# A graph layer on one core: edges sorted without gaps (831 gathers for 880 pairs), matmuls that find their chunk by registers, and a smaller routing sort

## What is computed

```python
def _hconv(x, W, b, src, dst, n):
    xt = x @ W
    m = segment_sum(xt[src], dst, n) * Binv[:, None]
    out = segment_sum(m[dst], src, n) * Dinv[:, None]
    return out + b
# graph part: two _hconv with a prelu; beside it a linear attention over all rows;
# behind both a normalization and a mixture of 8 experts, 2 of them weighted per row:
h = gelu(xn @ W1[e] + b1[e]); y += (h @ W2[e] + b2[e]) * w_full[..., e]
```

## Time and profile before

| | us |
|---|---|
| median of 3 runs | 6197.29 (6196.83 to 6203.05) |
| the profiled execution, time / span | 6198.35 / 6196.6 |
| mean granted TensorE clock | 0.841 |
| busy: PE / DVE / ACT / POOL | 4354.5 / 3632.5 / 1291.3 / 4050.3 |
| start to the first gather | 647 |
| pass 0, 1, 2, 3 with the stretch behind each | 1177, 1170, 1147, 1120 |
| normalization and scores | 237 |
| routing, of it the sort's loop | 157, 131 |
| experts, final sums | 470, 71 |

### The profile page before, as it was taken

One profiled execution on the slowest core, in us unless ns is written; L12 is line 12 of the kernel. 1 busy time (PEld: TensorE's weight loads), 2 busy tenths in 40 slices (PEclk: granted clock), 3 DMA queues, 4 the chain that ended last, 5 costly groups with the idle time before them and its releaser, 6 DMA issues.

```text
span 6196.6 us, 63953 instructions
## 1 busy us (share of the span) xinstructions
PE 4354.5 (70%) x16894; PEld 2841.8 (46%) x16895; DVE 3632.5 (59%) x10972; ACT 1291.3 (21%) x3391; POOL 4050.3 (65%) x4182
## 2 busy tenths in 40 slices
PE   4899799999957777675466565645565555647995
PEld 1555455555534444443244444424433333545663
DVE  7887788888846666665555555544444444443223
ACT  0587455555500000000100000000000000212442
POOL 2777777777757777777577777767777776003442
PEclk8999899999968888997777877777787776757997
DMA  3400333333353333334444444473333335200114
GB/s 116 126 1 1 85 104 104 103 103 103 104 127 112 112 112 111 112 112 94 131 137 139 136 137 138 128 191 109 105 105 105 105 105 98 90 27 29 61 62 158
DMA packets 331514, 641.97 MB, mean 104 GB/s; under 512 B 82320, under 2 KB 201700, under 8 KB 330704
## 3 DMA queue, kind: packets, MB, share of 16 engines
q0 software_dynamic: 191808, 490.67, 29.4%
q1 hardware_dynamic: 131652, 139.90, 6.9%
q10 hardware_dynamic: 7756, 7.97, 0.4%
HBM read 551.23 MB, written 87.01 MB: 103 GB/s over the span
## 4 chain that ended last, share of the span: by engine, by line
PE 46%; DVE 14%; issue 13%; POOL 8%; DMA 8%; ACT 1%; DVEq 1%; ACTq 0%; SPq 0%; POOLq 0%; PEldq 0%
PE PS L1367 27%; POOL gbuf L538 8%; DVE acc L946 7%; DMA gbuf<-table,idx 7%; PE PS L1335 6%; PE PS L1544 3%; PE PS L1567 3%; PE PS L1397 2%; DVE ohg L955 2%; PE PS L1524 1%; PE PS L1560 1%; PE PS L1435 1%; DMA gbuf<-ye_d 1%; PE PS L1492 1%; DVE gbuf L1194 0%
## 5 line engine op out<-in xcount | busy, mean ns | idle before, releaser
L538 POOL DMA_INDIRECT gbuf<-table,idx x3520 | 3364.4, 956 | 1184.1 <-issue 810.6
L1367 PE MATMUL PS<-gbuf,ohg 128*128 128x257 f32 (+1 forms) x7040 | 2273.6, 469 | 1383.0 <-issue 760.4
L1367 PEld LDWEIGHTS PS<-gbuf,ohg 128*128 128x128 f32 x7040 | 1539.5, 231 | 2108.3 <-issue 1323.4
L946 DVE TENSOR_TENSOR acc<-acc,PS 128x257 f32 (+1 forms) x3520 | 1492.8, 424 | 1715.2 <-PE PS L1367 1692.8
L955 DVE TENSOR_SCALAR ohg<-iota,dl 128x128 f32<-128x128 f16 x2640 | 813.7, 315 | 86.4 <-issue 86.4
L1335 PE MATMUL PS<-region 128*128 128x440 f16 x3328 | 687.3, 349 | 0.0
L546 POOL DMA_INDIRECT scattered_d<-acc x384 | 373.7, 973 | 127.1 <-issue 121.0
L1335 PEld LDWEIGHTS PS<-region 128*128 128x128 f16 x3328 | 324.5, 97 | 282.7 <-issue 1.6
L640 ACT ACTIVATE region<-region,acc 128x128 f16<-128x128 f16 x832 | 334.0, 401 | 522.6 <-DVE region L897 516.3
L896 DVE TENSOR_SCALAR region<-iota_c,acc 128x880 f16<-128x880 f16 x832 | 411.0, 494 | 23.2 <-issue 23.2
L1335 PE MATMUL PS<-acc,region 128*128 128x440 f16 x1792 | 335.3, 350 | 7.7 <-ACT region L641 7.7
(11 more groups left out here) (284 smaller groups left out, 3570.6 us busy)
## 6 DMA issues: line engine op xcount, KB each, us to landing
gbuf<-table,idx POOLq DMA_INDIRECT x3520, 2.8
table<-acc SPq DMA_DIRECT2D x21, 896.0 KB, 6.7
region<-xt_d SPq DMA_DIRECT2D x98, 128.0 KB, 2.2
gbuf<-ye_d SPq DMA_DIRECT2D x12, 1024.0 KB, 7.6
xpad_d<-acc SPq DMA_DIRECT2D x1, 6272.0 KB, 22.0
xn_d<-acc SPq DMA_DIRECT2D x49, 128.0 KB
xt_d<-acc SPq DMA_DIRECT2D x49, 128.0 KB
table<-acc SPq DMA_DIRECT2D x49, 128.0 KB
```

The source lines that it names most:

```text
L538: gp.indirect_dma_start(gbuf[:, c % U, 0:F], None, tables[p], bass.IndirectOffsetOnAxis(idx[p % 2][:, c:c + 1], 0)).then_inc(s_g[c % U // ...
L946: TT(a, a, chunk_sum(p, k), ALU.add).then_inc(s_acc[p], 1)
L1367: m = MM(chunk_sum(p, k), ohg[:, k, :], gbuf[:, k, 0:width(p)], start=True, stop=True)
```

## The change

- A block no longer begins a new chunk. Edges lie without gaps: CH = 831 chunks. A chunk in which a new block begins is used once for each block; such a use is a pair. Pair w reads chunk w minus the number of blocks begun before it; there are 879 at most, PAIR = 880. Gathers run over CH, one-hots, matmuls and adds over PAIR.
- The lane numbers per pair are made on the chip: transposes, a spreading by matmul (`stairs`, `turn_keys`, `spread_keys`, `lanes`), for order 0 ahead of pass 0, for order 1 in the last turns of pass 0.
- Gathered rows go to a ring of 58 (passes 0, 2) or 64 (1, 3) columns that takes `gbuf` and space of the idle accumulator. TensorE finds a pair's chunk by a register, 16 loaded per turn.
- Gather c waits (from c = ring on) for the add of pair c - ring + 48. Pair w waits for gather w, whatever chunk it reads. SyncE forwards landings: it waits for each group of 4 gathers and increments `s_arr`; GpSimd waits for that too, 8 groups back. SyncE's other work in the passes stands between these waits.
- The next accumulator is zeroed only behind the last add of a pass.
- The sort's fields become fp16 bit patterns (12500 needs no split); columns of the sort's matmuls are 416 instead of 440; the scattered word is split at bit 13.
- The routing sort carries the code alone, in fp16, column by column with two buffers of 7; the weight is applied in the final sums. `fold_beta` goes: the bias of all experts is made in one PSUM tile of 8 rows, written to DRAM and read back to all lanes. `w2` and this are loaded by ScalarE's queue after pass 3.

```diff
-    NC = -(-((E + NB * (P - 1)) // P) // U) * U
+    CH = -(-E // P)
+    NC = -(-CH // U) * U
+    PAIR = -(-(CH + NB - 1) // U) * U
+    RINGS = (58, 64)
+    RING_AT = (NB, 0)
+    BEHIND = NB - 1
...
+            def arrivals(p, j):
+                for n in range(j, min(j + U // AG, NAG)):
+                    sp.wait_ge(s_g[n % AS], landed(p, n))
+                    sp.sem_inc(s_arr[p], 1)
...
-                for c in range(NC):
-                    pool.wait_ge(s_acc[p], c + 1)
-                    gp.indirect_dma_start(gbuf[:, c % U, 0:F], None, tables[p],
+                for c in range(CH):
+                    if c % AG == 0 and c >= AG * AS:
+                        pool.wait_ge(s_arr[p], c // AG - AS + 1)
+                    if c >= ring:
+                        pool.wait_ge(s_acc[p], U + (c - ring + BEHIND + 1))
+                    gp.indirect_dma_start(rowset[:, at + c % ring, 0:F], None, tables[p],
...
+            for p in range(1, 4):
+                pool.wait_ge(s_acc[p - 1], U + PAIR)
+                pool.wait_ge(s_idx, 2)
+                memset_acc(p)
+                pool.wait_ge(s_tab, p * 16 * NR7)
+                gather_pass(p)
...
+            for i in range(NAG // (U // AG)):
+                if i < NB:
+                    if i:
+                        sp.wait_ge(s_st, i * 32)
+                    sp.dma_start(mx["xt"], ...)
+                    sp.dma_start(mx["xb"], ...)
+                    sp.dma_start(mx["xnb"], ...)
+                arrivals(2, i * (U // AG))
+                if i < NB:
+                    sp.wait_ge(s_res, i + 2)
+                    sp.dma_start(resid_d[i * P:(i + 1) * P, :], mx["rs"]).then_inc(s_st, 16)
+                    sp.dma_start(skip_d[i * P:(i + 1) * P, :], mx["sk"]).then_inc(s_st, 16)
...
                 for i in range(start, end):
+                    slot_of = slots_of(p, i)
                     for k in range(U):
                         if k % IB == 0:
-                            pe.wait_ge(s_g[k // IB], (i + (p * TURNS + 1)) * (IB * 16))
+                            pe.wait_ge(s_arr[p], min((i * U + k) // AG + 1, NAG))
-                        m = MM(chunk_sum(p, k), ohg[:, k, :], gbuf[:, k, 0:width(p)], start=True, stop=True)
+                        m = MM(chunk_sum(p, k), ohg[:, k, :], rowset[:, ds(slot_of[k], 1), 0:width(p)].rearrange("p a f -> p (a f)"), start=True, stop=True)
...
+            def next_lanes(i, k):
+                if (i, k) == (SORT_TURNS, 8):
+                    unpack(1)
+                if (i, k) == (SORT_TURNS, 12):
+                    stairs(1)
+                if (i, k) == (SORT_TURNS + 1, 12):
+                    lanes(1)
...
-                TT(fc["ohv"][:, :, 1, :], fc["ohc"], wide(wt.rearrange("p j b -> p (j b)"), NCE), ALU.mult).then_inc(s_eopen, 1)
+            for c in range(NK):
+                if c >= 2 * ES and c % ES == 0:
+                    dve.wait_ge(s_eused, c // ES - 1)
+                at = c % (2 * ES)
+                TS(fc["ohs"][:, at, :], iota_h[:, :], fb_["slot"][:, c:c + 1], None, ALU.is_equal)
+                m = TS(fc["ohv"][:, at, :], iota_c[:, 0:NCE], fb_["chunk"][:, c:c + 1], fb_["val"][:, c:c + 1],
+                       ALU.is_equal, ALU.mult)
...
-                link(TT(x2, x2, yl[q % 2][0:m, 0:n, 0, :], ALU.add))
-                TT(x2, x2, yl[q % 2][0:m, 0:n, 1, :], ALU.add).then_inc(s_add, 1)
+                for j in range(2):
+                    for b in range(n):
+                        x2 = accs[1][0:m, q * G + b, 0:F]
+                        a = STT(out=x2, in0=yl[q % 2][0:m, b, j, :], scalar=wt[0:m, j, q * G + b:q * G + b + 1], in1=x2,
+                                op0=ALU.mult, op1=ALU.add)
```

More of the change, by code:

```diff
@@ L216, in gps_layer @@
         nega = small[:, 7, 0:1]
+        row_number = small[:, 7, 1:2]
+        opens = [small[:, 7, 2 + o:3 + o] for o in range(2)]
+        sums, whole = small[:, 7, 4:6], small[:, 7, 6:7]
         stats7, mv7 = sb("stats7", [P, R7, 6], f32), sb("mv7", [P, R7, 2], f32)
-        nch_i = sb("nch_i", [P, 2], i32)
-        bw = sb("bw", [P, NW], f32)
-        bw_i = sb("bw_i", [P, NW], i32)
+        tot_i = sb("tot_i", [P, 6], i32)
+        bw = sb("bw", [P, 4, NW], f32)
+        bw_i = sb("bw_i", [P, 3, NW], i32)
         x_sb = acc_flat[1][:, 0:NB * F].rearrange("p (b f) -> p b f", f=F)
@@ L932, in _ @@
                     sort_column(0, i, k)
+            dve.wait_ge(s_openc, 2)
             unpack(0)
+            stairs(0)
+            turn_fields(0)
+            lanes(0)
             def block_numbers(p, i):
```

486 lines of the change are left out of this document (303 added, 183 removed).

## The result

The changed kernel takes 5993.33 us (median of 4 runs, 5990.35 to 6002.86), the kernel before 6200.07 us (4 runs, 6196.83 to 6203.05): a ratio of 0.9669, with an interval from 0.9653 to 0.9686. It is faster, by 207 us; 5993 had been predicted. The profiled execution has a span of 5990.2 us, 206.4 less than before. That the total was met to a microsecond is luck: of nine terms four are within 2 us, and the misses of the others, up to 14 us each, cancel. Ratios leave out runs over 1.5% above the fastest of their kernel, which matters in the last experiment alone, for three runs of eleven.

The account below looks back on a forecast made before the run. POOL's gathers were taken to bound all four passes. Passes -131, memset +10, start +1, routing sort -94, final sums +5 and second-layer weights +5 make -204: from 6198.4, less 1 more, about 5993 us; range 5930 to 6065.

Parts of the forecast that it names:

- Gathers: Four passes: 49 fewer gathers each, saving 62.8 us in pass 0, then 61.3, 61.6 and 61.3.
- Tails: Behind each pass's last gather: 52 pairs with no gather beside them, +37, +26, +22 and +21 us in passes 0 to 3.
- The memset: Between passes: started behind the last add, it holds a one-element tensor_scalar behind pass 1, +10 us; behind pass 0, 0.
- Ring and SyncE: Passes: ten pairs of lead suffice; +6 us once in pass 0 for a late start, +3 in pass 2 for SyncE's queue.
- rival (b): Passes 0 and 2: constant wait and ten pairs of lead bind, 1 us in each of 104 turns, 6085 us; chance 0.08.
- Routing sort: Routing sort: 131 us become 98 columns of two small fp16 compares, 35 plus 2 us; -94 us.
- Normalization: After pass 3: second-layer weight loads meet the first loads of skip and residual, +5 us, bounds 0 and +15.
- Experts: Expert loop: PE is back to back, so the ACT scaling that goes was hidden; 0 us.
- Final sums: Final sums: two adds per group become eight narrow ones with the weight, half exposed; +5 us, bounds 0 and +10.
- (a): Tails and transitions: clock stays high, DVE sets the tails, the memset holds nothing; 5950 us, chance 0.17.
- (c): Pass 0: PE loses its clock and the kernel gets slower, 6280 us at clock 0.75; chance 0.05.
- (d): Tails: PE at the lower clock, 0.94 us per pair, and a last landing of 10.5; 6060 us, chance 0.10.

Follow-up runs that it names:

- the last experiment: Changed kernel with later memset, pass 2's output matmuls behind pair 3 and expert weights loaded by GpSimd's queue: 7413.48 us, ratio 0.9929 to the kernel before, slower chip.
- e_static: Changed kernel with TensorE reading ring slots by constants, without register loads in the passes (sums of other rows): 6050.98 us.
- e_hold: Changed kernel, memset waiting for VectorE's reciprocals (and negated slope behind pass 1): last add to first gather 23.8 and 41.0 us, for 34.0 and 51.3.
- e_credit: Kernel before, with the first 16 gathers of a pass no longer waiting for TensorE's increment: 6190.55 us beside 6202.88.
- e_mix3: Changed kernel, pass 2's output matmuls moved from behind pair 4 to behind pair 3: pass 2's gathers 1234.8 us, repeat 1242.5, both on slower chips.
- e_w2pool: Changed kernel, experts' second weights and first bias loaded by GpSimd's queue instead of ScalarE's: last add to the end 843.2 us, for 852.4.
- e_scale: Changed kernel with ScalarE's copy of the expert's output back in the expert loop, factor 1: 6000.22 us.

## Why the prediction was right, point by point

**Gathers.** 49 fewer at 1.251 us: right in passes 1 and 3 (-61.4, -61.2). In pass 0 the forecast was 62.8 off and 6 on for a late start of TensorE, -57; measured -61.1. The late start is there: the first 80 gathers are 1.363 us apart, 6.3 us over the pass's mean, but in the kernel before they were 1.308, 2.0 over its own.

**Tails.** 52 pairs at 0.70 and 4.5 for the landing, 41 us: measured 40.5 and 38.3. Pass 1 41.7 for 45, pass 0 59.9 for 62. The landing of the last gather was taken too dear (4.5 us; it is forwarded 3.5 to 3.7 us behind the gather's start, for the row-0 padding beside which it took 10.5 is nearly gone), and a group of two hardly dearer than one of four. The price of TensorE's register load, 0.4 us per turn, came from the earlier trace rows, and there it was the wrong cause: in the changed kernel the loop still loads the registers and has no long iteration. e_static does not confirm the number either, for its tails lie within the spread of kernels that leave the passes alone. That 0.70 came out right is thus in part luck: four pairs take 2.37 us, 0.59 each, and the extra 0.75 at each turn's start is 0.05 per pair.

**The memset.** Half right. The hold was foreseen, behind pass 1 alone and on L1040; in fact the first tensor_scalar behind the last add takes it, L983 of before, and that one stands behind pass 0 as well. I had looked at the new memset there and not at the form of the old operation next to it. The step that put the 0-to-1 transition at 0, looking at the new memset alone, is the one that failed: 7.9 us net, a hold of 10.2. e_hold gives both back, 10.2 and 10.3 us.

**The stretch behind pass 1** was 10.5 us better than forecast by a wait that I did not list among the removed: gather c's wait for add c - 16 starts from TensorE's own increment. e_credit shows it.

**Ring and SyncE.** "It fits with 1.3 us to spare" for pass 2: it did not. The loop was worked out without the output matmuls inside the group of pairs 4 to 7, 1.9 us at a clock of 0.50, though they stood in the code: the group takes 5.10 us, where 1.9 to 3.75 had been set. SyncE's forwarding, for which no row stood, was set at 0.3 and takes 0.03. The gathers of this pass became only 47.0 us shorter, for 61.6 forecast, and for this loss of 14.6 +3 had been set. So rival (b) named the place and overpriced it: one gather in a turn waits about 0.3 us, in one pass, not 1 us in each turn of two. That it is TensorE and not SyncE that comes last is read from the loop's parts and supported by e_static; the edit that would show it, e_mix3, could not be read.

**Routing sort.** 35 + 2 against 38: right, -91.8 for -94 in the stage. Two compares are 0.38 apart, of the 0.33 to 0.4 given.

**Normalization.** +13 for +5, inside the bounds, by another mechanism: no meeting of loads, but ScalarE held 14.1 us by an issue. That e_w2pool returned it is shown.

**Experts.** -9.6 for 0: the step "PE is back to back in it, so ACT's scaling that goes was hidden" failed. It was back to back in three iterations of four, and the earlier trace rows show the fourth with a gap that I had put down to the registers. e_scale returns 5.7 us.

**Final sums:** +5.8 for +5.

**Rivals.** (a) came true in one half (clock 0.90 to 0.97 in the tails), not in the other (the hold was there twice). (c): no, pass 0's clock went from 0.98 to 0.99 with a register load in each turn. (d): no, a pair of pass 3's tail took 0.71 us in all and the last landing 3.5.

## What to carry to other kernels

A wait has two sides: before a change drops or rewrites one, list what else raises that semaphore, and when it first does, for the credit given at the door of a stage is a wait too. A bulk memset on GpSimd cost nothing beside two-tensor operations and its whole length to the first tensor_scalar on VectorE; let it start behind the small operations, not ahead of them. When a loop is back to back but for one iteration in four, ask what waits there before pricing the nearest instruction. And a wait's place is found by adding up the loop behind it part by part, with all that its engine does in between.

## What the runs showed of the hardware that was not expected

A tensor_scalar of 128x49 took 10.59 and 10.66 us beside a memset of 10.59, and 0.20 without; a reciprocal of 128x49 took its 0.47 beside one. An indirect gather on GpSimd took 2.00 us instead of 0.95 when it was issued 0.02 us behind the start of a tensor_tensor of 1024 columns with two SBUF inputs; 92 gathers of one variant lost 74.3 us beside such operations; the section of the Trainium skill named above gives such a lock against a GpSimd operation that reads SBUF; that the gather is held because it reads its indices there is argued, not shown. A DMA issue on ScalarE's queue took 14.12 us directly behind one of 4 MB, and 0.58 in the same place on GpSimd's. And on three of four chips of these experiments the kernels were 19 to 24% slower, with VectorE and TensorE standing still for several us at a time while gathers or scatters ran, and these running at their usual 0.95 us; the expert loop, which has indirect transfers too but is a loop and not written out, was not slower. Nothing in the profile names the cause, and it stays open.
